# Cross attention of a decoder layer: loops written out, the next token block prepared inside the steps, one key stack, another order of loads

## What is computed

```python
def interfere(x):
    return x + 0.1 * amp[0] * jnp.einsum('bhsdi,hij->bhsdj', x, interference)
qh, kh, vh = (interfere(qh), interfere(kh), interfere(vh))
scores = jnp.einsum('bhqdm,bhkdm->bhqkm', qh, kh) / math.sqrt(dk)
weights = jax.nn.softmax(scores, axis=3)
out = jnp.einsum('bhqkm,bhkdm->bhqdm', weights, vh)
...
x = x + _L0_xattn_ref(_layernorm(x, axis=-1), ctx_4096, ctx_4096, ...)
```

## Time and profile before, and how to read it

| | us |
|---|---|
| median of three executions | 3557.63 |
| the profiled execution | 3559.21 |
| its span | 3557.5 |
| TensorE busy in the span | 3379.9 (95%) |
| weight loads of TensorE | 2639.5 (74%) |
| VectorE, ScalarE, GpSimd busy | 1512.2, 1213.7, 1167.6 |
| cross attention, 2032.5 to 3209.3 | 1176.8 |

### The profile page before, as it was taken

One profiled execution on the slowest core, in us unless ns is written; L12 is line 12 of the kernel. 1 busy time (PEld: TensorE's weight loads), 2 busy tenths in 40 slices (PEclk: granted clock), 3 DMA queues, 4 the chain that ended last, 5 costly groups with the idle time before them and its releaser, 6 DMA issues. The chain is left out here.

```text
span 3557.5 us, 50266 instructions
## 1 busy us (share of the span) xinstructions
PE 3379.9 (95%) x17716; PEld 2639.5 (74%) x17716; DVE 1512.2 (43%) x2413; ACT 1213.7 (34%) x2478; POOL 1167.6 (33%) x655
## 2 busy tenths in 40 slices
PE   6999999999999999999999789979979989998999
PEld 5788887888887788877778567767757767773587
DVE  3232342323333232432323246656666675662453
ACT  3223242322332232232322145555555554550100
POOL 4334343343434334343434222333333332330000
PEclk9999999999999999999999889989989999988999
DMA  4323344233424323342322167766776767744142
GB/s 170 121 94 118 106 142 149 100 113 106 148 97 154 121 94 119 130 160 77 98 74 88 57 218 194 217 198 198 213 221 173 201 202 239 193 132 160 36 136 77
DMA packets 165144, 501.94 MB, mean 141 GB/s; under 512 B 20384, under 2 KB 20384, under 8 KB 165032
## 3 DMA queue, kind: packets, MB, share of 16 engines
q1 hardware_dynamic: 155816, 466.76, 41.7%
q10 hardware_dynamic: 9216, 33.56, 2.6%
HBM read 416.35 MB, written 83.89 MB: 141 GB/s over the span
## 5 line engine op out<-in xcount | busy, mean ns | idle before, releaser
L437 POOL TENSOR_TENSOR sa_wl<-sa_wraw,sa_wh 128x1024 fp32r<-128x1024 f32 x192 | 458.1, 2399 | 776.6 <-ACT sa_wh L588 776.6
L53 PE MATMUL sa_u<-sa_ln_xh,sa_wh 128*128 128x512 f32 x1536 | 628.3, 409 | 4.4 <-DVE sa_ln_xl L246 4.4
L54 PE MATMUL sa_u<-sa_ln_xl,sa_wh 128*128 128x512 f32 x1536 | 599.9, 391 | 0.0
L55 PE MATMUL sa_u<-sa_ln_xh,sa_wl 128*128 128x512 f32 x1536 | 599.5, 390 | 0.0
L1016 POOL TENSOR_TENSOR ca_probs<-ca_probs,ca_inv 128x512 f32<-128x512 f32 x256 | 263.7, 1040 | 750.8 <-DVE ca_inv L1368 750.8
L448 POOL TENSOR_TENSOR sa_pl<-sa_praw,sa_ph 128x1024 fp32r<-128x1024 f32 x128 | 317.8, 2513 | 443.5 <-ACT sa_ph L641 443.5
L53 PE MATMUL sa_pr<-sa_ph,sa_oh 128*128 128x512 f32 x1024 | 428.4, 418 | 0.1
L739 DVE TENSOR_TENSOR sa_acc<-sa_pr,sa_acc 128x512 f32<-128x512 f32 x256 | 176.3, 690 | 539.6 <-PE sa_pr L55 539.6
L54 PE MATMUL sa_pr<-sa_pl,sa_oh 128*128 128x512 f32 x1024 | 400.7, 391 | 0.0
L55 PE MATMUL sa_pr<-sa_ph,sa_ol 128*128 128x512 f32 x1024 | 400.0, 391 | 0.0
L53 PEld LDWEIGHTS sa_u<-sa_ln_xh,sa_wh 128*128 128x128 f32 x1536 | 289.4, 188 | 83.4 <-issue 24.1
(11 more groups left out here) (174 smaller groups left out, 5338.7 us busy)
## 6 DMA issues: line engine op xcount, KB each, us to landing
sa_wraw<-in_wqkv SPq DMA_DIRECT2D x192, 512.0 KB, 3.6
sa_praw<-in_wproj SPq DMA_DIRECT2D x128, 512.0 KB, 3.5
ca_wh<-w_folded_hi SPq DMA_DIRECT2D x96, 512.0 KB, 5.7
ca_wl<-w_folded_lo SPq DMA_DIRECT2D x96, 512.0 KB, 6.5
ca_kstack<-k_parts SPq DMA_DIRECT2D x192, 128.0 KB, 4.4
ca_qstack<-q_parts SPq DMA_DIRECT2D x96, 256.0 KB, 4.0
ca_owraw<-in_wo SPq DMA_DIRECT2D x32, 512.0 KB, 4.0
sa_nat<-in_w_nat SPq DMA_DIRECT2D x24, 512.0 KB, 4.7
```

What stands on the lines that cost most here:

```text
L53: nc.tensor.matmul(out, ah, bh, start=(first and i == 0), stop=False)
L54: nc.tensor.matmul(out, ah, bl, start=False, stop=False)
L55: ins = nc.tensor.matmul(out, al, bh, start=False, stop=(last and i == len(parts) - 1))
L437: nc.gpsimd.tensor_tensor(wl[:, u % 3], wraw[:, u % 3], f32(wh[:, u % 3]), ALU.subtract).then_inc(w_split, 1)
```

## The change

- The loops are written out: 33 steps in a row on each engine (`CrossStep`). Buffers and group numbers are constants; the copy of the biases to `bias_now` goes.
- `ca_ch` and `ca_cl` have two buffers. In each step of a block one chunk of the next block's context is loaded (one raw buffer; for block 0 `acc` serves) and split at the step's end by ScalarE and GpSimd.
- x of the next block is loaded in steps 1 and 2, its statistics are computed in steps 2 to 5, the square root in step 5, and it is normalised in steps 6 and 7, two tiles in each.
- The first two of the eight groups of transposes stand in step 7 and use `ca_o_ps`; six stay in step 0. They come in another order (first the left half of all four tiles), so that the query unit waits for four of them first and for all eight only in its middle.
- There is one key stack. It is filled after `scores(3)` of the running attention.
- SP's order: next key weights go ahead of the `kh` store, key stacks between the query stores; after a block, the stores of x2 and the loads of `acc` are spread over two steps.

```diff
+        self.more = self.proj and self.b < BLOCKS - 1
+        self.first = self.g == 0 and self.proj
+        self.closing = self.attn and self.attn_g == CH - 1
+        self.last = self.g == CH - 1 and self.more
...
-        ch = sb("ca_ch", [P, KC, BT], F32R)
-        cl = sb("ca_cl", [P, KC, BT], F32R)
-        craw = sb("ca_craw", [P, CRAW, BT])
+        ch = sb("ca_ch", [P, 2, KC, BT], F32R)
+        cl = sb("ca_cl", [P, 2, KC, BT], F32R)
+        craw = sb("ca_craw", [P, BT])
...
-        kstack = sb("ca_kstack", [PARTS * PC, 2, PAIRS, 2, BT], F32R)
+        kstack = sb("ca_kstack", [PARTS * PC, PAIRS, 2, BT], F32R)
...
+        def raw_context(b, k):
+            return craw[:] if b else acc[:, k // 2, (k % 2) * HALF:(k % 2 + 1) * HALF]
+        def turn_bank(i, b):
+            if b and i < EARLY:
+                return o_ps
+            return [x_ps, o_ps][i % 2]
...
+            def load_context(b, k):
+                if b:
+                    sp.wait_ge(c_split, b * KC + k)
+                sp.dma_start(raw_context(b, k), tile_of(ctxT, b * KC + k)).then_inc(c_loaded[k], 16)
...
+            def store_x2(s, t):
+                sp.wait_ge(x_free, s.m * PR + (2 * t + 3))
+                sp.dma_start(tile_of(x2, s.attn_b * TILES + t), acc[:, t]).then_inc(x2_stored[t], 16)
+            def load_acc(b, t):
+                sp.wait_ge(x2_stored[t], b * 16)
+                load(b, acc, acc_loaded, [t])
...
+            for s in STEPS:
+                after_closing = s.n > CH and s.g == 1
+                if after_closing:
+                    store_x2(STEPS[s.m], TILES - 1)
+                if s.attn and s.proj:
+                    next_weights(STEPS[s.m], 2)
+                if s.more:
+                    load_context(s.b + 1, s.g)
+                    if s.g in (1, 2):
+                        sp.wait_ge(ln.turned, s.b * ln.GROUPS + ln.GROUPS)
+                        load(s.b + 1, ln.x, ln.loaded, [2 * s.g - 2, 2 * s.g - 1])
                 if not s.attn:
-                    load(0, acc, acc_loaded)
+                    sp.wait_ge(c_split, KC)
+                    load(0, acc, acc_loaded, range(TILES))
                 if s.proj:
                     sp.wait_ge(ow_split, s.n + 1)
                     sp.dma_start(owraw[:], tile_of(wo, s.g)).then_inc(owraw_loaded, 16)
+                    next_weights(s, 0)
                     sp.wait_ge(u_hi, s.n * 2 + 1)
                     sp.dma_start(k_parts[0], f32(kh[:])).then_inc(k_hi_stored, 16)
                     sp.wait_ge(u_free, s.n * U + 3)
                     sp.dma_start(k_parts[1], f32(kl[:])).then_inc(k_lo_stored, 16)
-                    sp.wait_ge(kstack_zeroed, 1)
+                    if after_closing:
+                        load_acc(s.b, TILES - 1)
+                    if s.attn:
+                        sp.wait_ge(s_done, s.m * TILES + TILES)
+                    else:
+                        sp.wait_ge(kstack_zeroed, 1)
                     sp.wait_ge(k_hi_stored, s.n * 16 + 16)
-                    stack_keys(s.par, 0, k_parts[0])
-                    stack_keys(s.par, 2, k_parts[0])
-                    sp.wait_ge(k_lo_stored, s.n * 16 + 16)
-                    stack_keys(s.par, 1, k_parts[1])
-                    next_weights(s, 0)
+                    stack_keys(0, k_parts[0])
                     sp.wait_ge(u_hi, s.n * 2 + 2)
                     sp.dma_start(q_parts[0], f32(qh[:])).then_inc(q_hi_stored, 16)
+                    stack_keys(2, k_parts[0])
                     sp.wait_ge(u_free, s.n * U + 4)
                     sp.dma_start(q_parts[1], f32(ql[:])).then_inc(q_lo_stored, 16)
-                    if s.attn:
-                        sp.wait_ge(s_done, s.m * TILES + TILES)
+                    sp.wait_ge(k_lo_stored, s.n * 16 + 16)
+                    stack_keys(1, k_parts[1])
                     sp.wait_ge(q_hi_stored, s.n * 16 + 16)
                     stack_queries(0, q_parts[0])
                     stack_queries(1, q_parts[0])
                     sp.wait_ge(q_lo_stored, s.n * 16 + 16)
                     stack_queries(2, q_parts[1])
                     next_weights(s, 1)
-                if s.norm:
-                    load_context(s.b + 1, range(CRAW, KC))
-                if s.proj:
-                    next_weights(s, 2)
-                if s.cross or not s.proj:
-                    for t in range(TILES):
-                        sp.wait_ge(x_free, s.m * PR + (2 * t + 3))
-                        sp.dma_start(tile_of(x2, s.attn_b * TILES + t), acc[:, t]).then_inc(x2_stored[t], 16)
-                if s.cross:
-                    for t in range(TILES):
-                        sp.wait_ge(x2_stored[t], s.b * 16)
-                        sp.dma_start(acc[:, t], tile_of(x1_by_i, s.b * TILES + t)).then_inc(acc_loaded[t], 16)
-            pipeline(sp, first_block, step)
+                if s.closing:
+                    if s.proj:
+                        store_x2(s, 0)
+                        store_x2(s, 1)
+                        load_acc(s.b, 0)
+                        store_x2(s, 2)
+                        load_acc(s.b, 1)
+                        load_acc(s.b, 2)
+                    else:
+                        for t in range(TILES):
+                            store_x2(s, t)
...
+                if s.more:
+                    context_low(s.b + 1, s.g)
...
+                bank = turn_bank(i, b)
+                pe.wait_ge(ln.normal, b * TILES + (t + 1))
+                if b and i < EARLY:
+                    pe.wait_ge(o_split, m * TILES + (i + 3))
+                elif i >= EARLY + 2 or (i >= 2 and not b):
+                    pe.wait_ge(ln.lo_done, b * ln.GROUPS + (i - 1))
+                elif b:
+                    pe.wait_ge(x_free, m * PR + (i - EARLY))
...
+                        if u == 0 and s.first:
+                            pe.wait_ge(c_split, s.b * KC + (k + 1))
+                        if u == 1 and s.first and k % 4 == 0:
+                            pe.wait_ge(ln.lo_done, s.b * ln.GROUPS + (k + 4))
...
-                        if s.cross:
+                        if s.first:
                             pe.wait_ge(ln.lo_done, s.b * ln.GROUPS + ln.GROUPS)
+                    elif t >= 2 and s.last:
+                        pe.wait_ge(ln.lo_done, (s.b + 1) * ln.GROUPS + (t - 1))
...
                 scores(0)
-                turn_x(0)
-                turn_x(1)
                 pieces(0)
-                turn_x(2)
+                turn_now(2)
                 pieces(1)
-                turn_x(3)
+                turn_now(3)
                 pieces(2)
-                turn_x(4)
                 turn_v()
                 pieces(3)
-                turn_x(5)
+                turn_now(4)
                 pieces(4)
-                turn_x(6)
-                pieces(5)
-                turn_x(7)
-                pieces(6)
+                turn_now(5)
+                pieces(5, 6)
                 scores(1)
-                pieces(7, 8)
+                turn_now(6)
+                pieces(7)
+                turn_now(7)
+                pieces(8)
                 turn_probs(0)
...
                 pieces(17, 18)
+                turn_early(0)
                 project(1, 0)
...
                 project(2, 0)
+                turn_early(1)
                 turn_probs(3)
...
                 out_weights()
-                exps(0, 0, 1)
-                high_x(4, 5, 6, 7)
+                high_now(2)
+                exps(0, 0)
+                high_now(3)
+                exps(0, 1)
+                high_now(4, 5, 6)
                 high_unit(0, kh, k_hi_stored, k_lo_stored)
+                high_now(7)
                 exps(1, 0)
                 copy_probs(0)
...
                 exps(3, 1)
+                high_early(0)
                 copy_probs(2)
                 high_o(2)
-                if s.norm:
-                    ln.deviations(act, s.b + 1)
-                next_context(0, 1)
+                high_early(1)
                 copy_probs(3)
-                next_context(2)
                 high_o(3)
-                next_context(3, 4, 5, 6, 7)
-            pipeline(act, first_block, step)
+                if s.more:
+                    context_high(s.b + 1, s.g)
+                    if s.g == 5:
+                        ln.deviations(act, s.b + 1)
...
+                def next_normal(i):
+                    if s.more and s.g >= 6:
+                        t = 2 * (s.g - 6) + i
+                        dve.wait_ge(ln.rstd_done, s.b + 2)
+                        nc.vector.tensor_scalar(ln.x[:, t], ln.x[:, t], ln.mv[:, t, 0:1], ln.rstd[:, t:t + 1],
+                                                ALU.subtract, ALU.mult).then_inc(ln.normal, 1)
...
                 tops(0)
-                low_x(0, 1, 2, 3)
+                next_stats(0)
+                next_inverse_deviations()
+                low_now(2, 3)
                 place_v()
-                low_x(4, 5, 6, 7)
```

(29 more changed lines are left out.)

224 lines of the change are left out of this document (112 added, 112 removed).

## The result

The changed kernel takes 3480.2 us (median of 4 runs, 3474.3 to 3482.6); the kernel before took 3559.2 in the same comparison. The ratio is 0.9777, 95% interval 0.9763 to 0.9791: some 79 us faster. Forecast were 3487.0 us and a range of 3464 to 3522. The profiled execution took 3474.34 us, its span is 3472.6.

A forecast was written before the change was run, and what follows sets the result against it. TensorE's queue was taken to bound the cross attention: of 107.3 us above the floor 69.5 would be won, with the first scores' wait together 71. From 3559.2 that gives 3488.2, set to 3487 us for the median; range 3464 to 3522.

The forecast's parts named there:

- The back jump: Outer loop's jump back: its two unexplained waits, 21.0 us, go, with the slow start of the two steps behind.
- Its rival: At the outer jump: the unexplained 21.0 us come from saturated DMA and stay with the slow starts; 3513 us, chance 9%.
- Straight code is fetched behind the work, and I book nothing for it.: Written-out loops, all steps: fetching straight code would not stall the work; nothing booked.
- The steady step: The 18 steps outside the crossings: no wait for the query stack, from 32.08 to 31.60 us each.
- a late key stack in every step: Rival, 28 steps: key stack's chain misses the first scores, 6.8 us each, 190 more, 3677 us; chance 5%.
- Crossing, items 1 to 3: Each block crossing, over its floor: transposes 3.2 us, normalise pieces 2.3, splits 2.6.
- items 2 and 3: Each crossing on VectorE: normalise pieces in steps 6 and 7, 2.3 us; six splits in step 0, 2.6 us.
- Crossing, item 4: Step 1 of a new block: SP's queue delays the next start, 5 us at two crossings, 1 at the third.
- the first rival: SP's queue after crossings: 5 MB ahead of keys not absorbed, 10 us more twice, 4 at the third; 3511, 14%.
- Step 1: The phase's step 1, starting after a 4.3 us wait, stays slow: 2.5 us over the floor.
- In front of the first scores: Before the phase's first scores: query unit needs four of eight splits, not all, winning its wait of 1.46 us.
- No score matmul with an unexplained wait over 2 us: Sign the forecast is right, at score matmuls: none has an unexplained wait over 2 us.

The follow-up runs named there:

- e2: The kernel before with only the outer loop over the blocks written out, the inner loop kept; 3542.7 us, ratio 0.9950.
- e1: The kernel before with both cross-attention loops written out as a straight program, same order; 3560.0 us, ratio 1.0008.
- e3: The kernel before, loops kept, with the next step's key weights issued ahead of kh's store instead of behind the key stack; 3532.5 us, ratio 0.9931.
- e4: The changed kernel with the next step's key weights put back behind the key stack; 3596.6 us, ratio 1.0109.
- e5: The changed kernel with SP's queue after a block reordered: value weights ahead of two x2 stores, x loads and acc reloads spread out; 3457.6 us, ratio 0.9712.
- e10: The kernel before, loops written out, key weights ahead of kh's store, query stores ahead of the second and third key-stack parts; 3508.7 us, ratio 0.9854.

## Why the prediction was right, and where its steps were off

Time and sign were right. By its steps, in the profiled execution, 1008.27 us where the forecast's working gives 1086.89 - 69.5 = 1017.4. One reading is off by 0.2 us and changes nothing: TensorE asks for the next scores at +31.6, not +31.4. Step by step:

- **The back jump.** Right, and shown by e2 (18 us for 21.0 and its after-effects). Its rival, that the saturated DMA holds TensorE whatever the code is, falls with e2.
- **"Straight code is fetched behind the work, and I book nothing for it."** This is the step that failed in its reason, though not in the sum. For TensorE itself it holds: no unexplained gap inside a step is longer than 0.5 us. But the packets cost time on the way of others. In e1 straight code gave all 20 us back, likely in part through them. In the changed kernel they still do their work, now within the slack: step 12 has no packet between 20 and 24 us from its start and issues the query stack at +23.1; in step 13 one comes in (the DMA view of 2496.1 to 2499.8 has one q8 packet, that of 2464.9 to 2468.6 none), two issues of the key stack take 2.27 us on SP instead of 0.91, and the query stack goes out at +24.4. The step stays 31.3 long. Rows of steps 12 and 13:

```profile
2465.30 0.91 SPq L949 DMA_DIRECT2D ca_kstack<-k_parts  x2
...
2467.67 2.40 SPq L952 DMA_DIRECT2D ca_qstack<-q_parts  x3
...
2496.52 2.27 SPq L949 DMA_DIRECT2D ca_kstack<-k_parts  x2
...
2500.28 1.94 SPq L952 DMA_DIRECT2D ca_qstack<-q_parts  x3
```

  The Trainium skill (Runtime: NRT & Kernel Launch, Instruction fetch mechanics) says that crossing into the next 16 KB of code is mostly hidden. By that rule straight code is nearly free. e1 speaks against it where the order of the loads leaves no room (53.6 us of waits before the scores, against 24.8 before besides the two jumps), as far as these waits are the packets'; the changed kernel agrees with it. Its other half, that a jump out of the window stalls, agrees for the outer jump (10.4 and 10.6 us); the inner jumps, with no code packet in a steady step of e2, show no stall.
- **The steady step.** The arithmetic was right (no wait, stores landing in 2.0 to 3.5 us), but I gave the new order only a small part, the 8.5 us over the floor in 18 steps. It is worth 28 us by itself (e3) and 116 in the changed kernel (e4). Where it lies shows in e3: the 18 steps are 11.7 us shorter, for the floor is lower too, and the steps 9, 10, 17, 18, 25 and 26 behind the crossings another 11.7. The 18 steps take 567.5 us, forecast 568.8: what the floor of 31.22 gives is taken up by the function table's load in steps 6, 14 and 22 (0.7 to 1.7 us each), which I had not seen, and by small waits. The rival "a late key stack in every step" (5%) is what e4 does, with the query stack in the key stack's place: (1114.9 - 1008.3) / 31 = 3.4 us a step, and more than the 2.5 from which the forecast let it turn the sign.
- **Crossing, items 1 to 3.** 8.1 us over 2 x 31.60 were forecast for steps 7 and 0 together, that is 71.3; measured 66.1. VectorE's normalise pieces take 0.8 us each, not 1.5. A mean of four had hidden two kinds, as the rows of before and after below show (duration min/median/max). The 66.1 are 3.7 us over 2 x 31.22, of which the eight transposes at 0.40 are 3.2; so nothing of the 4.9 us booked for VectorE's pieces and splits (items 2 and 3) shows beyond 0.5. Three times 5.1 is 15.4 us too much.

```profile
L221 DVE TENSOR_SCALAR ca_ln_x<-ca_ln_x,ca_ln_mv,ca_ln_rstd x4: 802/1764/1927, 2316.6 to 2321.8; 128x1024 f32<-128x1024 f32 x4
```

```profile
L1469 DVE TENSOR_SCALAR ca_ln_x<-ca_ln_x,ca_ln_mv,ca_ln_rstd x12: 783/804/968, 2249.5 to 2834.9; 128x1024 f32<-128x1024 f32 x12
```

- **Crossing, item 4.** 5, 5 and 1 us were forecast for steps 1 and 2 of the new blocks, 200.6 in all; measured 72.2 + 70.2 + 66.6 = 209.0, 8.4 more. The place was right and e5 shows it: in step 9 `kh`'s store goes out at +15.1 instead of the steady +10.6, since SP waits for stores of x2 first, and lands 10.8 us after that instead of the 6.0 of step 12, so the query stack goes out at +30.7 instead of +23.1. So it is the term for SP's queue that was too small; the first rival (SP's queue, 14%) had the mechanism and too large a size. Right in kind was what the Trainium skill says on ring order (DMA: Bandwidth & Descriptors, Queues, rings and completion order), cited there: the trace has the 10.8 us behind some 5 MB issued in the 9.5 us before, and 8.7 in e5 with fewer bytes ahead. In e5 TensorE did not wait for it.
- **Step 1.** 34.1 forecast, 33.3 measured.
- **In front of the first scores.** 1.5 us forecast; from the phase's first unit matmul to the first scores it is 40.83 us, before 42.94: 2.1 won. Another 3.2 us of the profiled executions' difference come from the self attention's end, which moves by some 8 us from run to run (2040.6 to 2048.2 in the runs here).

Sum: -15.4 + 8.4 - 0.8 - 1.3 = -9.1, which is 1008.3 against 1017.4. So the 3487 was near the 3480 partly since two terms off in opposite directions half cancelled.

Of the signs named ahead, step 9 as the longest and under 40 us and almost no wait in the steady steps came as said. Steady steps of 31.2 us lie under the 31.5 to 31.7, step 7 with 32.3 us under the 33. "No score matmul with an unexplained wait over 2 us" failed by its letter, with 5.6, 4.9 and 4.1 us; the landing times explain these waits.

How the 79 us divide, from medians of different comparisons, each with an interval of its own of 5 to 11 us to either side: the outer jumps 18 to 20; the order of the loads 28, and some 4 to 6 more by letting straight code pay; between e10 and the changed kernel another 27 (ratios 0.9854 and 0.9777), for the second context buffer, the early normalise, the single key stack and the rest of the change together. I did not take these apart. The waits that vanished there are those of the old crossing shown above (12.7 and 9.1 us in e10). Given up were some 20 us by SP's queue, which e5 brings back.

## What to carry to other kernels

Where stores, their reload and prefetches share one queue, put the prefetch ahead of the store that has time and never between the store and the reload that someone waits for; ask of each megabyte who lands behind it. Before loops are written out, look for a store or load on the path with no slack: in e1 the gain vanished, likely since code packets come in beside the transfers; test the two edits together, not only apart. A saturated stretch of DMA is no bound by itself: at 351 GB/s and 101% a step still ran within 0.5 us of its floor once the urgent transfers were issued first.

## What I had not expected of the hardware

- A wait at a step's start can cost more than itself: after waits of 1.6 to 3.2 us six of twelve steps of e1 began with a mean clock of 0.75 to 0.77 over 6.9 us, and the one compared above was 1.4 us longer by it; the other six, and the step behind a wait of 0.6, did not.
- A change of ScalarE's function table takes 1.28 us. A square root once a block costs two, and the second stands ahead of the next exponential, wherever that is; what stands behind it decides whether it shows.
- VectorE's normalise pass over 128x1024 and GpSimd's split of a context chunk take longer beside each other, one of them or both. At the first crossing before, three passes beside splits took 1.75 to 1.93 us, and the fourth, when GpSimd had finished at 2321.4, took 0.80; the splits beside them took 1.29, 1.40 and 1.71 us. At the second crossing the first pass took only 0.82, and the split that started during it 1.85. After, no chunk is split beside a pass, GpSimd at most normalises probabilities, and a pass takes 0.78 to 0.97. Taking the overlap away by itself was not tried.
- SP, which only issues, can lose 1.4 us in the middle of two issues while a code packet comes in: so in steps 5, 13, 18 and 30 of the changed kernel, which are the ones with a q8 packet between the issues of `qh`'s and `ql`'s store (1.1 us in step 18).
